# New interleaving tables for three batches in flight, in a 12-layer decoder kernel on one core

## The reference, cut to what matters

```python
x = _layernorm(x + attn(x))            # L0: recurrent, L1: latent, L2 and L3: 16 heads
x = _layernorm(x + xattn(x, ctx_1024)) # 77 context tokens
x = _layernorm(x + ffn(x))             # L0: 8 experts by routing, L1: fp4, L2: low rank,
                                       # L3: convolution, attention, 8 dense experts of width 512
```

## Time and profile before

| what | us |
|---|---|
| median of 3 runs | 5204.9 (5201.24 to 5205.48) |
| the profiled execution's own time | 5209.52 |
| its span, first to last instruction | 5207.7 |
| PE busy (matmuls) | 4587.0 |
| PE's weight loads busy (beside the matmuls) | 3376.0 |
| DVE busy | 3232.7 |
| ACT busy | 2312.4 |
| POOL busy | 1159.1 |
| mean granted TensorE clock, share of full speed | 0.938 |

### The profile page before, as it was taken

One profiled execution on the slowest core, in us unless ns is written; L12 is line 12 of the kernel. 1 busy time (PEld: TensorE's weight loads), 2 busy tenths in 40 slices (PEclk: granted clock), 3 DMA queues, 4 the chain that ended last, 5 costly groups with the idle time before them and its releaser, 6 DMA issues.

```text
span 5207.7 us, 128273 instructions
## 1 busy us (share of the span) xinstructions
PE 4587.0 (88%) x54601; PEld 3376.0 (65%) x54601; DVE 3232.7 (62%) x8209; ACT 2312.4 (44%) x4614; POOL 1159.1 (22%) x1289
## 2 busy tenths in 40 slices
PE   5668988999898989899898989899898989898877
PEld 4346756677676767676676767676676767676554
DVE  7654577655657575656657575756667575756542
ACT  3324545434544444444544444444544444444321
POOL 5552221212112121212112121212112121212110
PEclk7668989999999999999999999999999999999987
DMA  2131100012010101011010101011100101010000
GB/s 65 29 92 50 59 2 2 4 55 61 30 34 15 56 21 50 27 44 33 26 32 21 56 21 52 25 42 29 38 28 19 58 19 56 17 44 22 16 21 27
DMA packets 154183, 181.61 MB, mean 35 GB/s; under 512 B 62890, under 2 KB 82450, under 8 KB 152850
## 3 DMA queue, kind: packets, MB, share of 16 engines
q1 hardware_dynamic: 153618, 173.41, 11.2%
HBM read 162.50 MB, written 10.55 MB: 33 GB/s over the span
## 4 chain that ended last, share of the span: by engine, by line
PE 64%; DVE 15%; ACT 5%; POOL 4%; issue 2%; DMA 1%; SPq 1%; POOLq 0%; DVEq 0%
PE g_pair L2760 9%; PE g_pair L2745 9%; PE g_pair L1586 6%; DVE g_tops L1690 5%; PE g_pair L1613 5%; PE g_pair L1636 5%; ACT g_keys_exps L1666 3%; PE g_pair L1983 2%; PE g_pair L1973 2%; POOL g_x L1409 2%; PE g_pair L1598 2%; POOL g_rstd L1405 1%; PE g_pair L2047 1%; PE g_pair L1556 1%; PE g_pair L1647 1%
## 5 line engine op out<-in xcount | busy, mean ns | idle before, releaser
L1666 ACT ACTIVATE g_keys_exps<-g_pair 128x1024 f32<-128x1024 f32 (+1 forms) x768 | 746.9, 1018 | 650.3 <-PE g_pair L1613 649.2
L1690 DVE TENSOR_REDUCE g_tops<-g_pair 128x8 f32<-128x1024 f32 (+1 forms) x768 | 750.4, 1005 | 339.2 <-PE g_pair L1586 336.1
L1405 POOL TENSOR_TENSOR g_rstd<-g_rstd,minus_half 128x4 f32<-128x4 f32 x224 | 237.4, 1060 | 3037.4 <-DVE g_rstd L1391 3036.2
L2760 PEld LDWEIGHTS g_pair<-region,g_keys_exps 128*128 128x128 f32 x4096 | 512.2, 192 | 121.8 <-issue 111.8
L2745 PE MATMUL g_pair<-g_xT,region 128*128 128x512 f32 x1024 | 546.3, 615 | 8.1 <-ACT g_keys_exps L2773 4.1
L2760 PE MATMUL g_pair<-region,g_keys_exps 128*128 128x128 f32 x4096 | 549.9, 279 | 3.5 <-DVE g_base L2792 3.5
L1636 PE MATMUL g_pair<-g_keys_exps,g_v 77*32 77x128 f32 (+1 forms) x12288 | 434.8, 285 | 69.9 <-DVE g_tops L1690 62.1
L1613 PE MATMUL g_pair<-g_qa,g_keys_exps 32*77 32x128 f32 (+1 forms) x12288 | 449.9, 284 | 42.8 <-DVE g_o L1711 28.9
L1613 PEld LDWEIGHTS g_pair<-g_qa,g_keys_exps 32*77 32x77 f32 (+1 forms) x12288 | 386.0, 171 | 140.5 <-DVE g_o L1711 62.8
L1586 PE MATMUL g_pair<-g_keys_exps,g_qa 32*128 32x256 f32 (+1 forms) x6144 | 395.3, 372 | 89.9 <-ACT g_keys_exps L1666 76.3
L1636 PEld LDWEIGHTS g_pair<-g_keys_exps,g_v 77*32 77x32 f32 (+1 forms) x12288 | 325.6, 113 | 179.7 <-DVE g_tops L1690 123.2
(11 more groups left out here) (378 smaller groups left out, 8591.1 us busy)
## 6 DMA issues: line engine op xcount, KB each, us to landing
region<-L_w_in SPq DMA_DIRECT2D x512, 256.0 KB, 3.0
region<-xT_in SPq DMA_DIRECT2D x16, 256.0 KB, 2.8
z_scratch<-m_z SPq DMA_DIRECT2D x4, 1024.0 KB, 5.3
g_qa<-xT_in SPq DMA_DIRECT2D x16, 256.0 KB, 4.4
g_oT_sc<-z_scratch SPq DMA_DIRECT2D x64, 64.0 KB, 3.2
g_o<-x_in SPq DMA_DIRECT2D x16, 256.0 KB, 3.6
out<-g_x SPq DMA_DIRECT2D x16, 256.0 KB, 2.3
setup_weights<-prepared_in SPq DMA_DIRECT2D x1, 2589.5 KB, 10.9
```

What stands on the lines that cost most here:

```text
L1405: e.tensor_tensor(g.rstd[:, :], g.rstd[:, :], g.s["minus_half"], ALU.pow).then_inc(*b.gpsimd(st + " rstd"))
L1666: e.activation(g.p[0:nk, 2 * k:2 * k + 2, :, :].rearrange("p g u q -> p (g u q)"), b.pair[st][k][0:nk, :, :].rearrange("p r c -> p (r c)") ...
L1690: e.tensor_reduce(top_columns(g, k), src, AX, ALU.max).then_inc(*b.vector(f"{st} top {n} {k}"))
L2760: ins = e.matmul(bank[1][:, n * D:(n + 1) * D], g.gated_hid[:, x % 2, c, n * T:(n + 1) * T], weights.part(f"w2 {x}", c), start=c == n == 0 ...
```

## The change

The five strings of `ORDER` and the string `GIVEN` are replaced by others of the same lengths, with the same number of every digit. No instruction is added, removed or altered. What differs is between which steps of other groups a step stands, which of the four PSUM pairs a stage gets, and between which other DMAs a DMA is issued. The tables were laid by durations of operations: those of GpSimd's normalisation, and of changes of the tile shape on PE, were set anew to measured ones.

```diff
@@ -262,188 +262,188 @@
 ORDER = {
     "tensor": (
-        "00101010202010210201020000010001022020000100110010112121211121221211121222101021012002100022000200100001"
...
+        "00001012020102010021020020101000100000202010101010112121211121221211121212201012012002100022000200100100"
...
     "sync": (
-        "0000ba02aa12121102a1122baabaaaaaaabaaaaaaaaaaaaaaaaaaaaaaaaaaaaaaaaaaaaaaabbbbbbbbbbbbb00000bb00bbbbbbbb"
...
+        "000010ba012121a2a21ab21b2baaaaaaaaaaaaaaaaaaaaaaaaaaaaaaaaaaaaaaaaaaaaaaaabbbbbbbbbbbbb00000bbb00bbbbbbb"
...
 GIVEN = (
-    "00201111020313200322021103111311022003231022001221200302101102031120130211022300120021100123001022110223"
...
+    "23021102001123102211002300021112110002221320031021022300001311110223001221031200001322211002230021101002"
...
```

More of the change, by code:

```diff
@@ L270 @@
[L270 to L274, removed]
@@ new lines @@
+        "22110112021012210100202220100022022201200021010012122012211212111121222121112122121021002002020002220121"
+        "21211210110122220200212012122020202220200202220200021201102100001001001010011010010100110101000110110110"
+        "00110102012010220221221012001011010010111010201010110101212111000001011210210021010010120100010101100010"
+        "20020020001211101010220212112221211212221212112010100111201221012101012020020202000220202000222020101012"
+        "10221201222010102110010102021010001001100102000201000100201001000100200100100201001000001001020000010010"
@@ new lines @@
+        "10000010000212122111212121201020110110111001011012102011101100101110100011011201000110110010101011121102"
+        "01101211101012001001001002021010120000220210000100201121220100000202002220020002010120001020120112020201"
+        "01002120021021001011010010111010001011101000110110020122222101022010020020202212221201121122112102021121"
+        "12010201020111010112021001101202200020210120002202200200222120010220120202220220020222020002202220200022"
+        "02201010202022212201100210111102102110110221021012102101010102112212212212010020121101022111101010011101"
@@ new lines @@
+        "00122012102002020220002022001210102101121012100200222021221220120220102101021201010100101101000101110100"
+        "01011102120121011012202212212222012022121022100220222022011021002001000110100120001002010010201020100120"
+        "02120101000102002202002002102121021221021202010120221022122100122121001200200200200122112111222212121222"
+        "12121212001011100101001110100112021212212022012011001001102020002101002112212010012121211212212111212221"
+        "21112122210102102122020100002002002100120012021100121022121001210111012120012110112111210220210210020201"
@@ new lines @@
+        "21121121011012120210210210200121020102102102110210210201210000111011210102101120201211021111002020200002"
+        "02000202001201122211212112221211202002120020021010121121120212101021121022112100210120202022020020222020"
+        "00202220200021012010202011201110110121121101101120221021001202111212220212212202202022012202102120102220"
+        "22102101202022022212112212210100111022102101110202102201102101010102112212221221210220101101022102211101"
+        "01011101001101220200022020220002002012101012101210121202022200120212120202100112201202201010100101101000"
@@ new lines @@
+        "10111010001011012021020102121112022022202210102201021012002202020010011202200200221002001001010100012002"
+        "01011010210202121210100100202010212102120210221020212012021021202122122102201201200200200200122112111222"
+        "21212122212121212001010110010101110100112021210021221222011010100102020121001021102202010012121211212212"
+        "11121222121112122211010120122002220000000202001201202100021220121001021002101101212111201101212212110102"
+        "11012020121211211011101011102102201010210201021020021120102102102021211210011001011011021021202002021101"
@@ L450 @@
+    "13132101022110101321231023211012010310102201221123010123102203220321200221210012130012032212012300011210"
+    "12001121032112230000131102221113220011231223210103211010201102222002132120020121000200010013010001002301"
+    "2301220223230300")
 BATCH = {
```

299 lines of the change are left out of this document (138 added, 161 removed).

## The result

The changed kernel takes **5132.5 us** in the median (5128.8 to 5136.9), the kernel before beside it 5205.2: a ratio of 0.985, with an interval of 0.983 to 0.988. The sign was right and the size was not.

A forecast was written before the change was run, and what follows sets the result against it. PE's own work was taken as the bound. Terms of 15 + 6 + 2.5 + 2 + 0 = 25.5 us off the median of 5204.9 gave 5179.4, forecast as 5180 us, with an 80% range of 5148 to 5210.

The forecast's parts named there:

- batch starts: At 13 batch starts, fewer weight pieces ahead of xT shorten PE's waits and half-clock time: 15 us, from 0 to 38.
- the start: Behind the opening, group 0's earlier x lets the first transposes come near 393 us: 6 us, from 0 to 9.
- the short waits of the middle: PE's 160 us of waits in three kinds are reshuffled without clear sign: 0, with 12 us either way.
- What bounds the kernel: PE's own work sets the middle; gains come only from idle time, half clock and tile-shape switches.
- 1.1 us a piece: Price of each weight piece between store and xT at batch starts; 14 fewer pieces give 15.4 us.
- DVE's 13 us: At batch ends, less of other groups' work before the last normalisation: 13 us more off the xT waits, capped at 30.1.
- Giving back: At batch starts, other waits take back what the loads return: a quarter off 20 us; as rival 5194 to 5197, chance 0.23.
- The tail: Three of group 2's expert pieces leave group 0's final chain, 3.2 us shorter: 2.5 us, from 0 to 3.2.
- Tile shapes: Along PE's order, 29 fewer changes of tile shape between neighbouring steps at 0.06 us each: 2 us.
- the cap is reached: Rival: xT waits vanish nearly everywhere and the clock stays up, 48 us gained, 5156 us; chance 0.17.
- Nothing but the tile shapes: Rival: only the 29 shape changes are saved, waits at starts, opening and tail move elsewhere, 5203 us; chance 0.08.
- the exponentials decide: Rival: more middle rounds wait for exponentials and run at half clock, slower at 5218 us; chance 0.12.

The follow-up runs named there:

- `early_before`: Kernel before with the next batch's mask, dots, context and xT issued ahead of the finished batch's store: 5180.2 us, ratio 0.9933.
- `sp_after`: Kernel before with only SP's order string taken from the changed kernel: 5196.9 us, ratio 0.9966.
- `ends_dve`: Kernel before with the changed DVE and POOL orders only in 13 windows around the batch ends: 5192.9 us, ratio 0.9957.
- `ends_early`: Kernel before with the changed DVE and POOL orders at 13 batch ends, plus next batch's loads ahead of the store: 5174.8 us, ratio 0.9942.
- `middle_only`: Changed kernel with before's orders up to about 510 us and before's DVE and POOL orders at the 13 batch ends: 5174.5 us, ratio 0.9933.
- `pieces_behind`: Kernel before with the 20 weight pieces between store and xT moved right behind xT in SP's string: 5190.3 us, ratio 0.9959.

## Why the prediction was right and wrong

Three terms were mis-sized. The batch starts had 15 us, and all that the waits for `xT` cost is 30 to 35 (`early_before`); the start had 6, and is worth 14 to 22; the short waits of the middle had 0, and bring about 20.

**What bounds the kernel**: right. PE's own work sets it, and no run shows a gain of another kind than idle time and clock.

**Batch starts**: the mechanism was right and the size was not. SP's order gave 13 to 18 us alone, against 15 forecast, and the waits for `xT` fell to 15.9 us in `sp_after`, the "about 15" of the forecast, which named it for the whole change, where 1.8 us are left. That it came so near is in part luck: 1.1 us a piece is no steady price, as one piece alone made a load land 0.7 to 2 us later (last section). The step that failed is the treatment of DVE's 13 us: "13 us more that could come off the same waits, but the cap is near". I priced the chain of the last normalisations as an addition to SP's saving, and then cut it off. In fact the order at the batch ends alone removes 25 of the 30.1 us (`ends_dve`), and in the changed kernel all but 1.8 are gone. The cap of 30.1 us was the right number to take for the term. With the engine orders the waits fell to 2.5 us even with the pieces in front.

**Giving back**: I took a quarter off for it and gave it 0.23 as a rival. In `early_before` 30.1 us of waits removed made 30.1 us less idle time, and in the changed kernel the other short waits did not grow in sum. In `ends_early` a third of it came back. As the main effect it is refuted.

**The start**: 6 us forecast, 14 to 22 measured. The transposes were forecast near 393 and came at 392.4, but with an opening that ended 3.6 us later, so it was luck that the number fits: they gained 12 us against the opening's end where 8 were forecast. (One sum there is off by little: nine DMAs of 0.45 us behind 378 make 382.1 and not 382.6.) The idle time that went was 8.8 us, the forecast's upper end of 9. What was left out is the clock of the first 130 us, worth 8.4 us there. The row that told it stood in the profile's windows before: a granted clock of 0.80 from 372 to 500.

**The tail**: 2.5 us forecast, 0 measured. The step "3.2 us leave the chain" failed, since the pieces covered a wait for DVE's sums; the question of what is late next was not asked here.

**Tile shapes**: 2 us were forecast. No run has them alone, and 2 us can't be told from nothing.

**The short waits of the middle**: 0 with 12 either way; they give about 20 us in median. This step failed outright. Of the 20 us, idle time explains a part: `middle_only` idles for 6.9 us less than `sp_after`, times 1.22 is 8 us. The rest goes with a mean clock of 0.9402 against 0.9384, some 10 us by the fit, and its own uncertainty is about 5. Which steps do it stays open: my count of rounds with short cover (183 to 190, 61 to 56, 33 to 31) pointed neither way, and the waits on L1666 did grow, by 3 us, where those for maxima fell by 6.

**The rivals**: "the cap is reached" (0.17) was the nearest, and true for the waits; its 5156 fell short by what the opening and the middle gave beyond it. "Nothing but the tile shapes", "given back" as the whole account, and "the exponentials decide" are refuted by the table; the last one needed 21 us of new waits, and 3 came.

**The range**: it treated the clock as 5 us at five starts. By the fit it is 29 of 73 us.

## What to carry to other kernels

Price the clock beside the idle time of a PE-bound kernel: here, by the fit, idle time counts 1.22 us a us, and a change of the mean granted clock by 0.001 is 5 us. Look at the granted clock of each stretch before counting waits: the 130 us behind the opening had 0.80, and half of the 17 us won there was clock. When a transfer is late, follow what it waits for back through all queues: the store's last normalisation on DVE mattered more than the pieces queued between store and load. And when work is taken out of a chain, look at which wait it had been covering.

## What the hardware showed

- The granted clock was at half for 14 us with PE busy for 80% of it and no wait over 2.1 us (0.51 from 414 to 428 us in the kernel before). In the 14 us before it the clock was 0.98 and no wait was over 1.4 us.
- Executions of one kernel differ by their clock. Over the 52 of the kernel before, the granted clock ran from 0.933 to 0.942 and the spans from 5195 to 5227 us, falling by 2.9 us for each 0.001 of clock within this kernel, and 5.3 between kernels; why these differ I have not settled.
- A 256 KB load with 256 KB loads ahead of it in the same queue landed later: the median of `xT` was 4.4 us before, 3.3 with the pieces moved behind it, and 3.0 in the changed kernel. Start by start in the kernel before: 2.9 to 3.0 us with no piece between store and load, 3.7 to 5.0 with one, 4.3 to 5.3 with two, 5.0 with three, 6.0 with five. It isn't the whole of it: with none between, `pieces_behind` still has 2.8 to 4.5.
